# A decoder layer with a state-space scan: a new order of the work ahead of the first scan, a second chunk's front that TensorE runs four slots ahead, and gate products four scans later

## The chip, the cores and the metric

One core of one Trainium2 chip. The metric is the device time of one execution in microseconds (us), the median of several; lower is better. Engines in the profile: PE is TensorE (PEld its weight loads), DVE is VectorE, ACT is ScalarE, POOL is GpSimd, SP is SyncE, which here only issues DMAs.

## The reference, cut to what matters

The layer is a Mamba-like state-space block, a cross-attention over 1601 context rows, and a mixture of experts. The change lies in the first block alone, which computes for 2048 tokens of width 256:

```
xz = layernorm(x) @ W_in                    # 256 -> 2 x 512
x_proj, z = split(xz)
x_conv = silu(conv4(x_proj) + conv_b)       # causal, 4 taps, per channel
dt_in, B = split(x_conv @ W_x)              # 512 -> 16 + 16
dt = softplus(dt_in @ W_dt + b_dt)          # -> 512
h  = h * exp(dt * A) + dt * B * x_conv      # per token; 512 channels x 16 states
y  = h.sum(states) + x_conv * D
x  = x + (y * silu(z)) @ W_out
```

Everything is float32. The cross-attention and the experts follow, and start when this block has ended.

## The kernel before

`scan_block` cuts the 2048 tokens into four chunks of 512 (NQ). In each chunk the 512 x 16 recurrences are laid out as 64 tiles of 128 partitions x 512 tokens, so there are 256 scans in all, numbered t; one is a TENSOR_TENSOR_SCAN of VectorE (L569). Scan t needs `exp(dt*A)`, made by ScalarE into one of five PSUM banks (L466, `psA`), and the input `dt*B*x`, made by GpSimd in pairs of tiles (L298) into a ring of eight (`b_in`). Both read `rep`, in which 32 channels of dt and of u = dt*x are copied to four groups of 32 partitions by DMA: four DMAs of 128 KB for each of j = 0..3 (`spread`, L208), for every 16 scans. TensorE adds up the 16 states of a channel (`add_states`, L774, once for four scans, L771 at the first of four such groups) into the bank `psY`. After 16 scans VectorE multiplies the sum by silu(z): `gate(n)` (L526), placed after scan t with t % 16 == 2. The next group's first sum waits for the gate (`gated`), and four scans wait for the sum three groups back (`summed`), since `h` holds three groups.

The order on every engine is that of the program text; it is written by hand. Chunk q's front (normalization, transposes, the x half and the z half of W_in, convolution, x_ssm, step size, B) is cut into steps with a slot k each, and `front_time(q, k)` gives the scan t at which an engine meets the step; each engine has its own k for its part (PE_X, ACT_X, ...). Chunk 1's steps are squeezed to 3/5 slot each from t = 4 on.

Chunk 0 has no scans to hide behind and runs as a plain sequence ahead of the loop over t:

- VectorE: `moments(0)` (L497, L500), `normalize(0)` (L507), four small copies (`pick`, L534), the twelve convolution products (L540, two tiles of SBUF in, chained by a semaphore), `moments(1)`, `neg_a` (L550), then for m = 0..3 bias and -|v| (L554, L556) and, in pairs, `step_and_input` (L518, L520), which makes dt and u; then `normalize(1)`.
- ScalarE: `xnT` (L432), exp of a_log (L434), the x half's evacuations and first taps (L322, L440), silu (L444), xs (L446), exp and ln for the softplus (L450, L452), the evacuations of B (L334). The z half of chunk 0 is evacuated in the loop at t = 2, 3, 5, 6, and its silu, with two loads of activation tables, stands at t = 12 (L338).
- GpSimd: the deviation of chunk 0 (L261, L263), `conv_d` (L273), `skip_d` (L278), `pick_b` (L281), the deviation of chunk 1, and the DMAs of j = 3 of the first spread; SP issues those of j = 0, 1, 2.
- TensorE: transposes (L605), the x half of W_in (L610), x_ssm (L645), step sizes and B's products in turns through two banks (L655, L660), then the z half, then the loop.

Of the kernel before, what the change touches and what calls it, by code (L numbers as in the profile page):

```python
# [50 lines left out]
ACT_Z0, ACT_ZS0 = (2, 3, 5, 6), 12  # L51
# [64 lines left out]
def scan_block(nc, x, w, x_res, shared, following, load_next, clear_next, make_pad, ident, power, ps):  # L116
# [7 lines left out]
    with ExitStack() as ctx:  # L124
# [89 lines left out]
        def _(sp_):  # L214
            xv = x[0].rearrange("(n p) d -> p n d", p=P)
            sp_.dma_start(x_res[:, 0:CHT, :], xv[:, 0:CHT, :]).then_inc(x_in, 16)
            sp_.dma_start(w_in[:, :, 0:DI], w["W_in"][:, 0:DI].rearrange("(k p) n -> p k n", p=P)).then_inc(s_win[0], 16)
# [30 lines left out]
        def _(pool):  # L248
# [68 lines left out]
        def _(act):  # L317
# [12 lines left out]
            def evac_b(q, g):  # L330
# [159 lines left out]
        def _(dve):  # L490
            link, _n = chain(dve, dve_link, 0)

            def moments(q):
# [1339 lines left out]
```

## Time and profile before

| | us |
|---|---|
| median of 3 runs (763.28 to 764.29) | 763.36 |
| the profiled execution, whole | 771.62 |
| its span | 769.9 |
| first scan starts, from the span's start | 48.40 |
| last scan ends | 410.66 |
| VectorE busy over the span | 592.6 (77%) |
| GpSimd busy | 475.0 (62%) |
| ScalarE busy | 445.9 (58%) |
| TensorE busy | 642.0 (83%) |

The profiled execution is 8.26 us longer than the median of the runs; 1.72 us of that lie outside its span. Busy shares are means over stages with different limits, so the two stages that the change touches (up to 48.40 us, and the scans up to 410.66 us) are read by themselves. In the rows, the number in square brackets is idle time of the engine before the instruction, with what ended it.

### The profile page before, as it was taken

The numbers are of one execution on the slowest core, as the hardware profiler recorded it, in microseconds if no ns is written. First come the engines' busy times: TensorE is split into PE (matmuls) and PEld (weight loads), VectorE is DVE, ScalarE is ACT, GpSimd is POOL, SyncE is SP. The second block draws the span as 40 slices with busy tenths as digits, with TensorE's granted clock in tenths as the row PEclk, the third lists the DMA queues.
The fourth block names the chain that finished last, engine by engine and source line by source line (L and its number), as shares of the span: only waits on it lengthen the run. The fifth ranks groups of instructions, "written<-read, shape, count | busy, mean of one in ns | idle before, by whom it ended". The sixth has DMA issues, their size and how long they took to land. (4 is left out here: it accounts for less than half of the span.)

```text
span 769.9 us, 10453 instructions
## 1 busy us (share of the span) xinstructions
PE 642.0 (83%) x3130; PEld 402.0 (52%) x3130; DVE 592.6 (77%) x1040; ACT 445.9 (58%) x795; POOL 475.0 (62%) x391
## 2 busy tenths in 40 slices
PE   4589865997689964588888899999999978899991
PEld 2133212352133510044535898989998954688860
DVE  5886788889998999999887776778798876344328
ACT  2667699676987888758773445545454330344420
POOL 4169589978997999999872423333445445155650
PEclk9899995999769996588999999999999999899996
DMA  7093144315344452943323844533443132455318
GB/s 197 19 212 72 38 110 109 83 44 131 72 109 110 92 128 68 245 102 86 72 86 108 249 138 153 178 123 117 143 133 99 38 119 76 121 158 163 112 32 299
DMA packets 61604, 91.33 MB, mean 119 GB/s; under 512 B 13573, under 2 KB 46536, under 8 KB 61550
## 3 DMA queue, kind: packets, MB, share of 16 engines
q1 hardware_dynamic: 52366, 76.72, 37.8%
q0 software_dynamic: 3936, 8.72, 3.2%
q10 hardware_dynamic: 5248, 5.24, 1.9%
q8 instruction: 26, 0.43, 0.2%
q14 instruction: 28, 0.23, 0.1%
HBM read 36.54 MB, written 22.62 MB: 77 GB/s over the span
## 5 line engine op out<-in xcount | busy, mean ns | idle before, releaser
L298 POOL TENSOR_TENSOR b_in<-rep,b_rep 128x1024 f32<-128x1024 f32 x128 | 299.0, 2358 | 41.8 <-DVE h L569 34.7
L569 DVE TENSOR_TENSOR_SCAN h<-ps,hlast,b_in 128x512 f32<-128x512 f32 x256 | 306.7, 1265 | 17.2 <-ACT ps L466 10.2
L466 ACT ACTIVATE ps<-rep,neg_a 128x512 f32<-128x512 f32 x256 | 171.0, 684 | 42.5 <-DVE h L569 38.7
L774 PE MATMUL ps<-h,pick 128*32 128x512 f32 x512 | 80.8, 708 | 43.0 <-DVE h L569 42.6
L610 PE MATMUL ps<-xnT,w_in 128*128 128x512 f32 x128 | 69.3, 688 | 10.0 <-ACT xnT L352 4.1
L1081 POOL DMA_INDIRECT rows_by_token<-yt,yrow x46 | 44.7, 972 | 44.0 <-issue 26.3
L1220 DVE TENSOR_TENSOR p_lo<-ps,p_hi 128x512 fp32r<-128x512 f32 x64 | 35.2, 592 | 36.0 <-ACT p_hi L1092 34.9
L1488 PE MATMUL ps<-v_hi,p_hi 128*128 128x256 f32 x208 | 59.8, 288 | 1.2 <-DVE x_res L1343 1.2
L774 PEld LDWEIGHTS ps<-h,pick 128*32 128x32 f32 x512 | 10.7, 115 | 93.7 <-DVE h L569 83.3
L1488 PE MATMUL ps<-v_lo,p_hi 128*128 128x256 f32 x208 | 58.4, 281 | 0.0
L1488 PE MATMUL ps<-v_hi,p_lo 128*128 128x256 f32 x208 | 58.2, 280 | 0.0
L610 PEld LDWEIGHTS ps<-xnT,w_in 128*128 128x128 f32 x128 | 26.8, 220 | 52.2 <-issue 40.9
L1092 ACT ACTIVATE p_hi<-ps 128x512 fp32r<-128x512 f32 x64 | 30.0, 516 | 37.4 <-PE ps L1505 37.4
L1694 PE MATMUL ps<-w_exp,xT 128*128 x184 | 45.4, 391 | 0.0
L625 PE MATMUL ps<-xp,conv_d 128*128 128x512 f32 x96 | 43.8, 601 | 0.0
L1488 PE MATMUL ps<-c_hi,q_hi 128*128 128x512 f32 x96 | 41.0, 427 | 0.8 <-PEq L124 0.8
L1038 POOL DMA_INDIRECT rows_by_block<-xn,pos x32 | 31.9, 996 | 15.7 <-issue 10.9
L1457 DVE TENSOR_TENSOR ht<-sgt,ps 128x256 f32<-128x256 f32 x23 | 9.7, 421 | 40.5 <-ACT sgt L1185 40.5
L1062 POOL TENSOR_TENSOR attn_rstd<-attn_mv,eps 128x1 f32<-128x1 f32 x14 | 4.1, 291 | 58.3 <-DVE attn_mv L1213 58.3
L1488 PEld LDWEIGHTS ps<-v_hi,p_hi 128*128 128x128 f32 x208 | 39.1, 188 | 1.4 <-DVE x_res L1343 1.4
L1488 PEld LDWEIGHTS ps<-v_lo,p_hi 128*128 128x128 f32 x208 | 39.2, 189 | 0.0
L1488 PEld LDWEIGHTS ps<-v_hi,p_lo 128*128 128x128 f32 x208 | 39.2, 188 | 0.0
(265 smaller groups left out, 1325.8 us busy)
## 6 DMA issues: line engine op xcount, KB each, us to landing
rep<-dt_u SPq DMA_DIRECT2D x252, 128.0 KB, 2.4
mask_sb<-in_mask_BxSxS_ik_dram SPq DMA_DIRECT2D x16, 800.5 KB, 4.6
xt<-rows_by_block SPq DMA_DIRECT2D x23, 258.0 KB
rows_by_block<-pad SPq DMA_DIRECT2D x4, 1032.0 KB, 9.4
rows_by_token<-pad ACTq DMA_DIRECT2D x4, 1024.0 KB, 6.2
yb<-rows_by_token SPq DMA_DIRECT2D x4, 512.0 KB, 5.5
w_exp<-L_ffn_expert_gate_w_dram SPq DMA_DIRECT2D x15, 128.0 KB
w_exp<-n_L_ffn_expert_up_w_dram SPq DMA_DIRECT2D x15, 128.0 KB
```

The costliest lines, as they stand in the source:

```text
L298: pool.tensor_tensor(b_in[:, (t - 1) % NB:(t - 1) % NB + 2, :], u_rep[:, n % 2, j - 1:j + 1, :], b_rep[q % 2][:, g, :].unsqueeze(1).to_bro ...
L466: act.activation(psA[:, t % NDA, :], dt_rep[:, n % 2, j, :], ACT.Exp, scale=neg_a[:, k:k + 1]).then_inc(exp_ready, 1)
L569: dve.tensor_tensor_scan(h[:, QC * (s % NH) + j, :], psA[:, t % NDA, :], b_in[:, t % NB, :], hlast[:, k:k + 1], ALU.mult, ALU.add).then_in ...
L610: last = pe.matmul(psF[:, m % 2, :], w_in[:, n, part * DI + m * P:part * DI + (m + 1) * P], xnT[:, n, :], start=(n == 0), stop=(n == KE - 1))
L625: last = pe.matmul(psF[:, m % 2, :], conv_d[:, m, n, :], xp[:, m, n:n + CH], start=(n == 0), stop=(n == NTAP - 1))
L774: last = pe.matmul(psY[32 * j:32 * j + 32, :], pick[:, :], h[:, QC * (s % NH) + j, :], start=False, stop=(g == NG - 1))
L1038: pool.indirect_dma_start(xs_dram[:, :], bass.IndirectOffsetOnAxis(ap=pos[:, t, k:k + 1], axis=0), xn3[:, t, :], None, bounds_check=NTILE ...
L1081: pool.indirect_dma_start(y_dram[:, :], bass.IndirectOffsetOnAxis(ap=yrow[:, 2 * s + a:2 * s + a + 1], axis=0), yt[:, s % YT, a, :], None, ...
L1092: act.activation(p_hi[:, a:b, :], psP[g % 2][:, 0:(b - a) * P], ACT.Copy).then_inc(pthi_ready, 1)
L1220: dve.tensor_tensor(p_lo[:, a:b, :], psP[g % 2][:, 0:(b - a) * P], p_hi[:, a:b, :].bitcast(F32), ALU.subtract).then_inc(ptlo_ready, 1)
L1488: mm = pe.matmul(out, stat[a], mov[b], start=first and n == 0, stop=last and n == 2)
L1694: last = pe.matmul(psG[i % 2][:, a * 2 * FI:(a + 1) * 2 * FI], xT[:, i % 2, cols], w_all[:, ds(e, 1), wcols].rearrange("p a n -> p (a n)") ...
```

## The change

Ahead of the first scan:

- x of chunk 1 is loaded by a DMA of its own, third in SP's queue. `moments(1)`, `normalize(1)` and `neg_a` move ahead of the convolution on VectorE; GpSimd makes chunk 1's deviation ahead of `conv_d`, and waits for chunk 1's normalization before `conv_d`.
- TensorE does 36 transposes of the identity (WARM) before the first real ones.
- The z half of W_in follows the x half directly, in four banks of `psA`; its silu is taken from there by ScalarE between the silus of the convolution, so the evacuations, the silu and the two table loads of chunk 0 leave the loop.
- All four step sizes are computed in a row, into four banks. The softplus of m = 0, 1 is finished ahead of the loop; that of m = 2, 3 goes into the loop: VectorE's L554 and L556 after scans 1 and 2, ScalarE's exp and ln at t = 5 and 6, VectorE's `step_and_input` after scans 6 and 7.
- Of the first spread, SP issues two DMAs of j = 0 and those of j = 1 and 3, ScalarE two of j = 0, GpSimd those of j = 2 (after the second u). The first four inputs are made singly by GpSimd. B's four products go to four banks and are evacuated behind ScalarE's DMAs.

In the loop: chunk 1's front is placed at 7/10 slot a step from t = -4 on, and TensorE runs its steps another four slots earlier. `gate` stands after t % 16 == 6. The `after` lines of the diff use names new to it: `psV` are the four banks of the step sizes.

```diff
@@ -40,6 @@
 PE_LAST = 58
+GATE_AT = 6
...
@@ -48,7 @@
 ACT_Z, ACT_XS, ACT_BR, ACT_V, ACT_ZS = (39, 40, 42, 43), 49, (52, 53, 56, 57), (58, 60, 64, 66), 76
-ACT_Z0, ACT_ZS0 = (2, 3, 5, 6), 12
+POOL_J, PE_LEAD, WARM = 2, 4, 36
+LATE_ABS, LATE_EXP, LATE_STEP = (1, 2), (5, 6), (6, 7)
...
@@ -58,11 @@
 def front_time(q, k):
-    return 4 + k * 3 // 5 if q == 1 else TILES * (q - 1) - SHIFT + k
-def front_slots(t, first=1):
-    return [(q, k) for q in range(first, NQ + 1) for k in SLOTS if front_time(q, k) == t and (q > 1 or k >= 0)]
+    return k * 7 // 10 - 4 if q == 1 else TILES * (q - 1) - SHIFT + k
+def front_slots(t, first=1, lead=0):
+    return [(q, k) for q in range(first, NQ + 1) for k in SLOTS if front_time(q, k) == t + (lead if q == 1 else 0) and (q > 1 or k >= 0)]
...
@@ -168 @@
+        psV = [psF[:, 1, :], psF[:, 0, :], psY, psA[:, KM, :]]
...
@@ -215,6 @@
     sp_.dma_start(w_in[:, :, 0:DI], w["W_in"][:, 0:DI].rearrange("(k p) n -> p k n", p=P)).then_inc(s_win[0], 16)
+    sp_.dma_start(x_res[:, CHT:2 * CHT, :], xv[:, CHT:2 * CHT, :]).then_inc(x_next, 16)
...
@@ -227,8 @@
     sp_.dma_start(w_in[:, :, DI:], w["W_in"][:, DI:].rearrange("(k p) n -> p k n", p=P)).then_inc(s_win[1], 16)
-    sp_.dma_start(x_res[:, CHT:, :], xv[:, CHT:, :]).then_inc(x_rest, 16)
-    sp_.dma_start(w_out[:, :, :], w["W_out"].rearrange("(m p) n -> p m n", p=P)).then_inc(s_wout, 16)
+    sp_.dma_start(x_res[:, 2 * CHT:, :], xv[:, 2 * CHT:, :]).then_inc(s_rest, 16)
+    sp_.dma_start(w_out[:, :, :], w["W_out"].rearrange("(m p) n -> p m n", p=P)).then_inc(s_rest, 16)
...
@@ -238,8 @@
             sp_.wait_ge(b_ready, 16 * (n - 1))
-        for j in range(QC if n else QC - 1):
-            spread(sp_, n, j)
+        for j in range(QC):
+            if n == 0 and j == 0:
+                spread(sp_, n, j, range(0, 2))
+            elif n or j != POOL_J:
+                spread(sp_, n, j)
...
@@ -268,7 @@
     inverse_deviation(0)
-    pool.wait_ge(xn_ready, 1)
+    inverse_deviation(1)
+    pool.wait_ge(xn_ready, 2)
...
@@ -279,9 @@
     pool.tensor_copy(pick_b[:, :, :], pick[:, NS:2 * NS].unsqueeze(2).to_broadcast([P, NS, 32])).then_inc(pick_ready, 1)
-    inverse_deviation(1)
-    pool.wait_ge(u_ready, 1)
-    spread(pool, 0, QC - 1)
+    pool.wait_ge(u_ready, 2)
+    spread(pool, 0, POOL_J)
...
@@ -292,7 @@
             pool.wait_ge(rep_sem(n, j), rep_count(n, j))
-        if j % 2:
+        if t < QC:
+            pool.tensor_tensor(b_in[:, t, :], u_rep[:, 0, t, :], b_rep[0][:, 0, :], ALU.mult).then_inc(b_ready, 1)
+        elif j % 2:
...
@@ -331,7 @@
             act.wait_ge(b_ready, TILES * (q - 1))
-        act.activation(b_rep[q % 2][:, g, :], psF[:, (g + 1) % 2, :], ACT.Copy).then_inc(br_ready, 1)
+        act.activation(b_rep[q % 2][:, g, :], psF[:, (g + 1) % 2, :] if q else psA[:, g, :], ACT.Copy).then_inc(br_ready, 1)
...
@@ -439,28 @@
                        scale=conv_w[:, m, 0:1]).then_inc(tap_done, 1)
-    for m in range(KM):
+    def silu_x0(m):
         act.activation(xc[0][:, m, :], xc[0][:, m, :], ACT.Silu).then_inc(xc_ready, 1)
-    act.wait_ge(xs_ps, 1)
-    act.activation(xs[:, :], psF[:, 0, :], ACT.Copy).then_inc(xs_ready, 1)
-    act.preload_act_table_set("natural_log_exp_and_others")
-    for m in range(KM):
+    def silu_z0(m):
+        act.wait_ge(z_ps, m + 1)
+        act.activation(zs[0][:, m, :], psA[:, m, :], ACT.Silu).then_inc(z_evac, 1)
+    def log_step(m):
         act.activation(u[:, m, :], u[:, m, :], ACT.Ln, bias=1.0).then_inc(sp_ready, 1)
-        if m % 2:
-            evac_b(0, m - 1)
-            evac_b(0, m)
+    silu_x0(0)
+    silu_x0(1)
+    silu_z0(0)
+    silu_x0(2)
+    silu_z0(1)
+    silu_z0(2)
+    silu_x0(3)
+    silu_z0(3)
+    act.wait_ge(xs_ps, 1)
+    act.activation(xs[:, :], psF[:, 0, :], ACT.Copy).then_inc(xs_ready, 1)
+    act.preload_act_table_set("natural_log_exp_and_others")
+    for m in range(2):
+        log_step(m)
+    act.wait_ge(u_ready, 1)
+    spread(act, 0, 0, range(2, QC))
+    for g in range(NG):
+        evac_b(0, g)
     act.wait_ge(consts_ready, 1)
+    act.wait_ge(br_ready, NG)
             act.wait_ge(rep_sem(n, j), rep_count(n, j))
+        if t == KM:
+            act.wait_ge(v_evac, KM)
...
@@ -469,10 @@
                            h[:, QC * (e % NH):QC * (e % NH) + QC, CH - 1], ACT.Copy).then_inc(saved, 1)
-        if t in ACT_Z0:
-            evac_z(0, ACT_Z0.index(t))
-        if t == ACT_ZS0:
-            silu_z(0)
+        if t in LATE_EXP:
+            log_step(2 + LATE_EXP.index(t))
...
@@ -522,7 @@
         dve.wait_ge(summed, NG * (n + 1))
-        dve.wait_ge(zs_ready, q + 1)
+        if q:
+            dve.wait_ge(zs_ready, q)
+        else:
+            dve.wait_ge(z_evac, KM)
...
@@ -533,6 @@
     last.then_inc(pick_ready, 1)
+    moments(1)
+    normalize(1)
+    dve.wait_ge(a_exp, 1)
+    for r in range(QC):
+        rows = slice(32 * r, 32 * r + 32)
+        dst = neg_a[rows, :].rearrange("p (b g j) -> p b g j", b=KM, g=NG)
+        src = a_log[rows, :, :].rearrange("p (b j) (g n) -> p n b g j", b=KM, n=QC)[:, r]
+        last = dve.tensor_scalar(dst, src, -1.0, None, ALU.mult)
+    last.then_inc(consts_ready, 1)
...
@@ -541,23 @@
         last.then_inc(conv_done, 1)
-    moments(1)
-    dve.wait_ge(a_exp, 1)
-    for r in range(QC):
-        rows = slice(32 * r, 32 * r + 32)
-        dst = neg_a[rows, :].rearrange("p (b g j) -> p b g j", b=KM, g=NG)
-        src = a_log[rows, :, :].rearrange("p (b j) (g n) -> p n b g j", b=KM, n=QC)[:, r]
-        last = dve.tensor_scalar(dst, src, -1.0, None, ALU.mult)
-    last.then_inc(consts_ready, 1)
-    for m in range(KM):
+    def step_bias(m):
         dve.wait_ge(v_ps, m + 1)
-        dve.tensor_scalar(dt[:, m, :], psF[:, (m + 1) % 2, :], b_dt[:, m:m + 1], None, ALU.add).then_inc(v_evac, 1)
+        dve.tensor_scalar(dt[:, m, :], psV[m], b_dt[:, m:m + 1], None, ALU.add).then_inc(v_evac, 1)
         dve.scalar_tensor_tensor(u[:, m, :], dt[:, m, :], -1.0, dt[:, m, :], ALU.mult, ALU.min).then_inc(neg_abs, 1)
-        if m % 2:
-            step_and_input(m - 1)
-            step_and_input(m)
-    normalize(1)
+    step_bias(0)
+    step_bias(1)
+    step_and_input(0)
+    step_and_input(1)
...
@@ -568,7 @@
                                hlast[:, k:k + 1], ALU.mult, ALU.add).then_inc(scanned, 1)
-        if t % 16 == 2 and t > 16:
+        if t in LATE_ABS:
+            step_bias(2 + LATE_ABS.index(t))
+        if t in LATE_STEP:
+            step_and_input(2 + LATE_STEP.index(t))
+        if t % 16 == GATE_AT and t > 16:
...
@@ -652,12 @@
             pe.wait_ge(br_ready, NG * q + m + 3)
-        pe.matmul(psF[:, (m + 1) % 2, :], w_dt[:, m * P:(m + 1) * P], xs[:, :], start=True, stop=True).then_inc(v_ps, 1)
+        pe.matmul(psF[:, (m + 1) % 2, :] if q else psV[m], w_dt[:, m * P:(m + 1) * P], xs[:, :], start=True, stop=True).then_inc(v_ps, 1)
             pe.wait_ge(br_ready, NG * q + g - 1)
-        pe.matmul(psF[:, (g + 1) % 2, :], pick_b[:, QC * g:QC * g + QC, :].rearrange("p n d -> p (n d)"), xs[:, :],
+        pe.matmul(psF[:, (g + 1) % 2, :] if q else psA[:, g, :], pick_b[:, QC * g:QC * g + QC, :].rearrange("p n d -> p (n d)"), xs[:, :],
...
@@ -675,7 @@
         if k == PE_XNT:
-            pe.wait_ge(dt_ready, KM * q)
+            if q == 1:
+                pe.wait_ge(v_evac, 2)
+            else:
+                pe.wait_ge(dt_ready, KM * q)
...
@@ -776,38 @@
     pe.wait_ge(ident_ok, 2)
+    for _ in range(WARM):
+        pe.transpose(psA[:, KM, 0:P], ident[:, :], ident[:, :])
         x_part(0, m)
+    pe.wait_ge(s_win[1], 16)
+    for m in range(KM):
+        w_in_product(psA[:, m, :], m, 1).then_inc(z_ps, 1)
     small_product(0)
+    for m in range(KM):
+        step_size(0, m)
     pe.wait_ge(pick_ready, 2)
-    for m in range(KM):
-        if m == 2:
-            pe.wait_ge(br_ready, 1)
-        if m == 3:
-            pe.wait_ge(br_ready, 2)
-        step_size(0, m)
-        if m % 2:
-            pe.wait_ge(v_evac, m)
-            spread_b(0, m - 1)
-            pe.wait_ge(v_evac, m + 1)
-            spread_b(0, m)
-    pe.wait_ge(s_win[1], 16)
-    for m in range(KM):
-        if m < 2:
-            pe.wait_ge(br_ready, 4 - m)
-        else:
-            pe.wait_ge(z_evac, m - 1)
-        w_in_product(m, 1).then_inc(z_ps, 1)
+    pe.wait_ge(z_evac, KM)
+    for g in range(NG):
+        spread_b(0, g)
     pe.wait_ge(diag_ready, 2)
+    for t in range(-2 * PE_LEAD, 0):
+        for c, f in front_slots(t, 1, PE_LEAD):
+            front(c, f)
         q, k, s = t // TILES, t % TILES, t // QC
+        if t == QC:
+            pe.wait_ge(v_evac, KM)
             add_states(s - 1)
-        for c, f in front_slots(t):
+        for c, f in front_slots(t, 1, PE_LEAD):
...
```

## Rows read from the trace of the kernel before

**Rows 1.** The groups of VectorE's instructions, 48 to 400 us: count, busy, mean, idle before.
```profile
L569 DVE TENSOR_TENSOR_SCAN h<-ps,hlast,b_in 128x512 f32<-128x512 f32 x247 | 296.1, 1265 | 17.2 <-ACT ps L466 10.2 <-ACT hlast L470 3.6 <-POOL b_in L298 3.4
L526 DVE TENSOR_TENSOR zs<-ps,zs 128x512 f32<-128x512 f32 x15 | 10.1, 676 | 13.1 <-PE ps L774 13.1
```

**Rows 2.** The same view of GpSimd, 48 to 400 us.
```profile
L298 POOL TENSOR_TENSOR b_in<-rep,b_rep 128x1024 f32<-128x1024 f32 x127 | 296.6, 2358 | 41.8 <-DVE h L569 34.7 <-DMA rep<-dt_u 6.8
L314 POOL TENSOR_TENSOR dt_u<-dt_u,xc 128x512 f32<-128x512 f32 x12 | 15.2, 1267 | 4.1 <-DVE dt_u L584 4.1
```

**Rows 3.** Timeline of all engines, 0 to 62 us: start, length of the group, instruction, idle before.
```profile
4.45 1.41 DVE L497 BATCH_NORM_STATS2 stats<-x_res 128x6 f32<-128x256 f32 x4 [3.42 <-DMA x_res<-in_x_dram]
...
7.71 1.38 DVE L507 TENSOR_SCALAR xn<-x_res,mv,rstd 128x256 f32<-128x256 f32 x4 [1.45 <-POOL rstd L263]
9.01 4.99 DVE L534 COPY pick<-ident 32x32 f32<-32x32 f32 x4
9.17 3.61 POOL L273 TENSOR_TENSOR conv_d<-ident,conv_w 128x2048 f32<-128x2048 f32 x1 [1.50 <-DVE xn L507]
...
12.74 1.04 POOL L278 TENSOR_TENSOR skip_d<-ident,d_skip 128x512 f32<-128x512 f32 x1
...
14.07 0.61 POOL L281 COPY pick_b<-pick 128x512 f32<-128x512 f32 x1 [0.29 <-DVE pick L534]
...
17.72 9.04 DVE L540 SCALAR_TENSOR_TENSOR xc<-xp,conv_w,xc 128x512 f32<-128x512 f32 x12 [3.72 <-ACT xc L440]
...
27.57 1.93 PE L645 MATMUL ps<-xc,w_x 128*32 128x512 f32 x8 [6.14 <-ACT xc L444]
...
30.30 3.47 PE L655 MATMUL ps<-xs,w_dt 128*128 128x512 f32 x4 [0.80 <-ACT xs L446]
...
36.67 18.26 SPq L208 DMA_DIRECT2D rep<-dt_u  x28
...
48.40 14.21 DVE L569 TENSOR_TENSOR_SCAN h<-ps,hlast,b_in 128x512 f32<-128x512 f32 x12 [3.16 <-POOL b_in L298]
```

**Rows 4.** TensorE in one stretch: stretch and length, busy, granted clock, DMA share, GB/s.
```profile
27.00:28.00 1.00, 0.43 (x4) 0.50 0.00 0
```

**Rows 5.** From issue to landing: the spreads (36 to 62 us), then W_in's two halves.
```profile
DMA to landing us min/median/max: 2.4/3.6/5.4
...
DMA to landing us min/median/max: 4.8/4.9/5.0
```

**Rows 6.** VectorE's waits, 48 to 98 us, last row 98 to 130: total, times, longest.
```profile
DVE h L569 <- ACT ps L466: 4.9, 3, 3.7
DVE h L569 <- ACT hlast L470: 3.6, 1, 3.6
...
DVE zs L526 <- PE ps L774: 1.9, 1, 1.9
...
DVE dt_u L584 <- ACT dt_u L385: 4.9, 3, 2.5
```

**Rows 7.** Timeline, 60 to 98 us: tables and silu on ScalarE, TensorE's x_ssm product.
```profile
62.13 1.28 ACT L338 ACT_TABLE_LOAD   x1
...
96.77 1.04 PE L645 MATMUL ps<-xc,w_x 128*32 128x512 f32 x8
```

**Rows 8.** Timeline behind the scans: a GpSimd instruction beside and without VectorE's L1315.
```profile
424.74 2.33 DVE L1315 TENSOR_TENSOR v_lo<-v_all,v_hi 128x1024 fp32r<-128x1024 f32 x2
...
424.90 1.08 POOL L1062 TENSOR_TENSOR attn_rstd<-attn_mv,eps 128x1 f32<-128x1 f32 x1 [4.86 <-DVE attn_mv L1213]
...
462.54 0.19 POOL L1062 TENSOR_TENSOR attn_rstd<-attn_mv,eps 128x1 f32<-128x1 f32 x1 [4.18 <-DVE attn_mv L1213]
```

**Rows 9.** Timeline around three gates, VectorE and TensorE, from 145 to 362 us.
```profile
156.22 0.69 DVE L526 TENSOR_TENSOR zs<-ps,zs 128x512 f32<-128x512 f32 x1 [4.81 <-PE ps L774]
...
183.58 1.06 PE L774 MATMUL ps<-h,pick 128*32 128x512 f32 x8 [1.68 <-DVE h L569]
...
351.40 1.91 PE L771 MATMUL ps<-xc,skip_d 128*128 128x512 f32 x2
```

More of the change, by code:

```diff
@@ L169, in scan_block @@
         psA = ps[:, 3 * BANK:8 * BANK].rearrange("p (s n) -> p s n", s=NDA)
+        psV = [psF[:, 1, :], psF[:, 0, :], psY, psA[:, KM, :]]
         psL = [psF[:, 0, 0:DM], psF[:, 1, 0:DM]] + [psA[:, t % NDA, 0:DM] for t in (TILES * NQ - 5, TILES * NQ - 4)]
-        x_in, x_rest, s_win, s_small, s_zero, s_alog = sem("x_in"), sem("x_rest"), [sem("w_x_in"), sem("w_z_in")], sem("small_in"), sem("zeroed"), sem("alog_in")
+        x_in, x_next, s_win, s_small, s_zero, s_alog = sem("x_in"), sem("x_next"), [sem("w_x_in"), sem("w_z_in")], sem("small_in"), sem("zeroed"), sem("alog_in")
         pick_ready, diag_ready = sem("pick_ready"), sem("diag_ready")
-        s_conv, s_wout = sem("conv_in"), sem("w_out_in")
+        s_conv, s_rest = sem("conv_in"), sem("rest_in")
         ident_ok = sem("ident_ok")
@@ L200, in rep_sem, with spread @@
         def rep_sem(n, j):
-            return rep_pool if n == 0 and j == QC - 1 else rep_in[n % 2][j]
+            return rep_pool if n == 0 and j == POOL_J else rep_in[n % 2][j]
         def rep_count(n, j):
-            return (n // 2 + (0 if j == QC - 1 and n % 2 == 0 and n else 1)) * QC * 16
-        def spread(eng, n, j):
-            for r in range(QC):
+            return (n // 2 + (0 if j == POOL_J and n % 2 == 0 and n else 1)) * QC * 16
+        def spread(eng, n, j, rows=range(QC)):
+            for r in rows:
                 eng.dma_start(rep[32 * r:32 * r + 32, n % 2, j, :, :],
@@ L493, in moments @@
             def moments(q):
-                dve.wait_ge(x_in if q == 0 else x_rest, 16)
+                dve.wait_ge(*((x_in, 16), (x_next, 16), (s_rest, 32))[min(q, 2)])
                 dve.wait_ge(xn_ready, q)
@@ L543, in _ @@
                 last.then_inc(conv_done, 1)
-            moments(1)
-            dve.wait_ge(a_exp, 1)
-            for r in range(QC):
-                rows = slice(32 * r, 32 * r + 32)
-                dst = neg_a[rows, :].rearrange("p (b g j) -> p b g j", b=KM, g=NG)
-                src = a_log[rows, :, :].rearrange("p (b j) (g n) -> p n b g j", b=KM, n=QC)[:, r]
-                last = dve.tensor_scalar(dst, src, -1.0, None, ALU.mult)
-            last.then_inc(consts_ready, 1)
-            for m in range(KM):
+            def step_bias(m):
                 dve.wait_ge(v_ps, m + 1)
-                dve.tensor_scalar(dt[:, m, :], psF[:, (m + 1) % 2, :], b_dt[:, m:m + 1], None, ALU.add).then_inc(v_evac, 1)
+                dve.tensor_scalar(dt[:, m, :], psV[m], b_dt[:, m:m + 1], None, ALU.add).then_inc(v_evac, 1)
                 dve.wait_ge(v_evac, m + 1)
                 dve.scalar_tensor_tensor(u[:, m, :], dt[:, m, :], -1.0, dt[:, m, :], ALU.mult, ALU.min).then_inc(neg_abs, 1)
-                if m % 2:
-                    step_and_input(m - 1)
-                    step_and_input(m)
-            normalize(1)
+            step_bias(0)
+            step_bias(1)
+            step_and_input(0)
+            step_and_input(1)
             for t in range(TILES * NQ):
@@ L606, in normal, with w_in_product @@
                 last.then_inc(xnT_ps, 1)
-            def w_in_product(m, part):
+            def w_in_product(out, m, part):
                 for n in range(KE):
-                    last = pe.matmul(psF[:, m % 2, :], w_in[:, n, part * DI + m * P:part * DI + (m + 1) * P], xnT[:, n, :],
+                    last = pe.matmul(out, w_in[:, n, part * DI + m * P:part * DI + (m + 1) * P], xnT[:, n, :],
                                      start=(n == 0), stop=(n == KE - 1))
@@ L619, in x_part @@
                     pe.wait_ge(x_evac, m - 1)
-                w_in_product(m, 0).then_inc(x_ps, 1)
+                w_in_product(psF[:, m % 2, :], m, 0).then_inc(x_ps, 1)
             def convolve(q, m):
@@ L629, in project @@
                 pe.wait_ge(gated, KM * (q + 1))
-                pe.wait_ge(s_wout, 16)
+                pe.wait_ge(s_rest, 32)
                 for m in range(KM):
@@ L694, in front @@
                         pe.wait_ge(c_evac, 3 + m)
-                    w_in_product(m, 1).then_inc(z_ps, 1)
+                    w_in_product(psF[:, m % 2, :], m, 1).then_inc(z_ps, 1)
                 if k == PE_XS:
```

1 line of the change is left out of this document (removed).

## The prediction, written before the result was known

> **What bounds the kernel now.** The page's busy shares name no one engine, so the reader goes to the two stages that the change touches. The timeline of the first 62 us is a chain of single engines: normalization, convolution on VectorE from 17.72 to 26.76, x_ssm on TensorE at 27.57, step sizes at 30.30, then SP's first spread DMA at 36.67, where the first u is ready (36.64), and the first scan at 48.40, 11.76 us behind that u [rows 3]. From there to 410.66 us the groups by engine show VectorE at 296 us of scans and GpSimd at 297 us of inputs in 352 us [rows 1, 2]. GpSimd's idle time is 34.7 us of waiting for scans, so VectorE sets the pace; its spacing is 14.21/12 = 1.18 us a scan [rows 3]. What it loses is idle time: 13.1 us before gates, for TensorE's sums, 13.8 us for ScalarE before scans [rows 1]. The waits by stretch put 10.4 us of the loss between scans 8 and 24 (4.9 + 3.6 + 1.9) and 4.9 us, before the step sizes of chunk 1, between scans 37 and 42 [rows 6]. All else behind the scans shifts with them.
>
> **The sum** is made against the profiled execution, 771.62 us; the median is 8.26 lower.
>
> **1. Up to the first u: +0.9 us (0 to +1.8 as forecast, -3.9 if nothing collides).** VectorE's order becomes: copies, moments and normalization of chunk 1, neg_a, convolution. x of chunk 1 is issued third; W_in's half, issued just ahead of it, takes at most 5.0 us to land [rows 5], so it is there at about 8 us, ahead of its use. Moments start at about 9.6 us, and from moments to the normalization's start it takes 7.71 - 4.45 = 3.26 us, the normalization 1.38 [rows 3]: done at 14.2. neg_a (0.9 us, an estimate from the kernel's page of groups) ends at 15.1. Were the first taps ready then (TensorE is kept busy ahead by 36 transposes, and the x half's first product took twice the time of the later ones), the twelve convolution products, 9.04 us [rows 3], would end at 24.2 instead of 26.76.
>
> But conv_d now starts only when chunk 1 is normalized, at 14.3, and so runs to 17.9, with skip_d (1.04) and pick_b (0.61) behind it, beside the convolution; before they were over at 14.7, ahead of it [rows 3]. Does VectorE run beside GpSimd? A copy of 32x32 elements beside conv_d did not: four of them took 4.99 us while conv_d and skip_d ran [rows 3]. And GpSimd's L1062, 0.19 us alone, took 1.08 us when VectorE had a product of two SBUF tiles under way [rows 8]. The convolution's products read two SBUF tiles each. No row shows such a product waiting for GpSimd, so the bounds are no wait (end at 24.2) and a wait for all three instructions (17.9 + 1.65 + 9.04 = 28.6). I take the second, being nearest to both rows: +1.8 us.
>
> The Trainium skill (SBUF — State Buffer, "Who interferes with whom") says that a VectorE instruction with two SBUF inputs contends with a GpSimd instruction that reads SBUF, and that whichever came first holds the port for its whole length. By that rule the end is 28.6; without it 24.2. The rows agree with it from GpSimd's side.
>
> Behind the convolution, ScalarE's silu order puts chunk 0's z between, which is ready by then and costs nothing: the silu that x_ssm waits for comes when the last convolution block does. TensorE now has the z products to fill the wait; its x_ssm products ran at 0.5 granted clock (the 1.2 GHz level) after 6.14 us idle [rows 3, 4] and took 1.93 us, against 1.04 us later [rows 7]; the first step size took 1.73 (two of L655) where half would do. If the clock stays up, that is -0.9 - 0.9 = -1.8; TensorE is idle about 4 us instead of 6, so I take half: -0.9. Sum +0.9: the first u at 37.5.
>
> **2. From the first u to scan 8: +9.2 us (+2.6 to +10).** The first scan comes sooner. Before, scan 0 stood at u + 11.76. Now four DMAs of j = 0 go out on two queues at once, the first landing 2.4 us after its issue, four at about 4.6 (the fastest and the median of the spreads [rows 5] leave 3.6 to 5.4); one single input is 1.27 (as L314 [rows 2]): scan 0 at u + 6.0, a gain of 5.8. It is given back at once: all 16 DMAs still need until about u + 11, since they are as many bytes, so scans 1 to 3 wait for landings, two bias steps (2 x 1.4) fill the gaps, and scan 4 stands at u + 16.4, where it was before (u + 16.5). Then two step_and_input calls, 2.8 us, lie in the path after scans 6 and 7: scan 8 at u + 23.9 against u + 21.3. That is the lower end, +2.6. Each call has two products of two SBUF tiles with a semaphore between, GpSimd is in its pairs of 2.36 us, back to back, and up to eight inputs ahead; if each of the four lets one pair pass, or nearly (one finds GpSimd waiting), plus 0.7 for the bias step of m = 3, it is 2.36 x 2.5 + 0.7 = 6.6 more: u + 30.5. I take that, by the same reading as in step 1. Behind these waits: ScalarE and TensorE are ahead of VectorE there and gain room.
>
> **3. Scans 8 to 24: -10.4 us (-6.8 to -10.4).** The table load at 62.13 [rows 7] opens the z half's silu, 4.5 us with two loads, in the loop; it goes, and with it the 4.9 us of waits for ps. The gate that waited 1.9 us for TensorE stands four scans (4.7 us) later. The 3.6 us before scan 24 came when ScalarE, late for want of TensorE's convolution, did its own silu; TensorE is four slots ahead now. If only ScalarE's work counts, these 3.6 stay.
>
> **4. Scans 24 to 64: -1.6 us (0 to -3).** 7/10 slot a step gives ScalarE's step sizes 6 scans where they had 5: of 4.9 us of waits about 3.3 remain.
>
> **5. The gates from scan 64 on: -3.2 us (+6.1 to -11.2).** 13.1 - 1.9 = 11.2 us of gate waits lie there, 4.81 of them at one [rows 1, 9]. The gate four scans later covers each, but TensorE is busy without a break from 134 to 182 us, and ends with only 1.68 us to wait for VectorE [rows 9]: what the gate gains is lost before the residuals that need the same TensorE. So 1.7 us there, 0.4 in the next chunk, 1.1 at the last two gates.
>
> Sum: 0.9 + 9.2 - 10.4 - 1.6 - 3.2 = -5.1 us; 771.6 - 5.1 = 766.5 for a profiled execution, 758.3 for the median. I say 758.0.
>
> **The rivals.**
>
> A, nothing collides: VectorE's two-tile products run beside GpSimd. For it: no row shows them waiting. Against: rows 8, seen from the other side. Steps 1 and 2 are then -3.9 (2.6 us earlier convolution and 1.3 of clock, TensorE having no gap) and +2.6: 763.4 - 3.9 + 2.6 - 10.4 - 1.6 - 3.2 = 746.9. Chance 0.15.
>
> B, the later gate holds TensorE, which decides where TensorE and not VectorE sets the pace. Its sum of the next group waits for the gate; before, TensorE came to that point at 351.40, 2.3 us after the gate [rows 9]; four scans later the gate ends at 354.5, so TensorE loses 3.1 us there, and by the same reckoning 1.7 at scan 86 and 1.3 at scan 118. If these 6.1 us pass to the end in place of step 5's gain, the sum is 763.4 - 1.9 + 6.1 = 767.6, slower than before. For it: TensorE is the late one at five gates. Against: behind 351.40 TensorE waits for ScalarE anyway. Chance 0.13.
>
> C, chunk 1's front is bound by ScalarE, whatever slots it gets: step 3 gives 6.8 and step 4 nothing. 763.4 + 0.9 + 9.2 - 6.8 - 3.2 = 763.5. For it: ScalarE has 0.69 us of exp a scan and some 31 us of front in 64 scans, nearly VectorE's time. Against: silu and z of chunk 0, 6.8 us, leave it. Chance 0.13.
>
> The forecast has 0.59, with its own range 751 to 763. A difference below 0.2% (1.5 us) can't be told from none. Faster: 0.15 of A, 0.55 of the forecast, 0.05 of the others, 0.75; same: 0.10, most of it C; slower 0.15, B and what of the forecast meets with C. The range, 747 to 765, leaves out half of A and most of B.
>
> **What would show it.** In the new trace: conv_d at 14 us and the convolution's first product not before 17.9, its last at about 28.5 (A: first at 15, last at 24); x_ssm's eight products in about 1.0 us if the clock held; first scan at 43.5, with gaps before scans 1 to 3; the products of L518's step after scans 6 and 7 with 1 to 2.4 us of waiting each (A: none), scan 8 at about 68; no table load between 40 and 75 us and no gate that waits over 1 us; new waits of the residuals behind scans 73 and 137; TensorE idle before the first sum after each gate, 3 us or more. The first scan later than 48, or TensorE still late at the end of the block, would make the prediction wrong.

## The result and the profile after

The changed kernel takes **776.95 us** (median of 4 runs, 775.45 to 778.79), the kernel before 763.83 beside it: ratio **1.0146**, 95% interval [1.0123, 1.0169]. The two medians lie 13.1 us apart, the ratio is worth 11.2 us: slower, where 5 us less was forecast. The profiled execution is 778.79 us long, its span 777.1.

The first scans of successive groups, from timelines of VectorE, show where the time went (us; the last column is the change of the stretch):

| scan | before | after | stretch | change | forecast |
|---|---|---|---|---|---|
| 0 | 48.40 | 44.80 | | | |
| 8 | 57.83 | 70.04 | start to 8 | +12.2 | +10.1 |
| 24 | 88.19 | 89.83 | 8 to 24 | -10.6 | -10.4 |
| 64 | 147.43 | 146.94 | 24 to 64 | -2.1 | -1.6 |
| end of 255 | 410.66 | 421.11 | 64 to end | **+10.9** | **-3.2** |

The stretch behind the last scan is 359.2 us in the profile before and 355.9 after. Its code is unchanged, and it differs between the profiles of this case (352.9 to 362.5 us), so positions of scans are compared below where a few us matter, and medians for verdicts.

**From scan 64 on.** VectorE's waits from 147 us to the last scan: total, times, longest.

```profile
DVE x_res L542 <- PE ps L670: 11.4, 6, 2.8
DVE h L603 <- ACT ps L496: 8.9, 9, 1.7
DVE dt_u L622 <- ACT dt_u L394: 6.4, 4, 3.2
```

The same view of the kernel before, 147 to 411 us:

```profile
DVE zs L526 <- PE ps L774: 11.2, 4, 4.8
DVE h L569 <- ACT ps L466: 4.3, 6, 1.7
DVE dt_u L584 <- ACT dt_u L385: 2.0, 3, 1.2
```

The gate waits of [rows 1] are gone. In their place stand the residuals (11.4 us), and VectorE's waits for ScalarE are 9 us larger: 27.4 us of waiting in all instead of 17.5. TensorE's own waits over the same stretch (150 to 421 us) name what made the projections and step sizes late:

```profile
PE ps L812 <- DVE zs L557: 36.9, 9, 6.9
PE ps L815 <- DVE h L603: 20.6, 10, 4.8
```

Before it was 5.3 us in 4 waits (the line below, of that kernel's TensorE, 147 to 411 us). TensorE starts a group's sum with two skip_d products (L812) into the one bank that the gate reads. They wait for the gate, and TensorE runs in order.

```profile
PE ps L771 <- DVE zs L526: 5.3, 4, 2.2
```

One such chain, in timelines of TensorE, ScalarE and VectorE of the changed kernel, 290 to 304 us (start, length of the group, instruction, idle before):

```profile
293.35 2.08 PE L812 MATMUL ps<-xc,skip_d 128*128 128x512 f32 x2 [5.78 <-DVE zs L557]
...
297.22 2.07 PE L693 MATMUL ps<-xs,w_dt 128*128 128x512 f32 x2
...
300.33 1.12 PE L693 MATMUL ps<-xs,w_dt 128*128 128x512 f32 x2
```
```profile
299.33 0.69 ACT L389 ACTIVATE dt_u<-ps,b_dt 128x512 f32<-128x512 f32 x1 [3.39 <-PE ps L693]
...
301.15 0.63 ACT L394 ACTIVATE dt_u<-dt_u 128x512 f32<-128x512 f32 x1
```
```profile
292.63 0.67 DVE L557 TENSOR_TENSOR zs<-ps,zs 128x512 f32<-128x512 f32 x1
...
301.81 0.69 DVE L622 TENSOR_TENSOR dt_u<-ps,dt_u 128x512 f32<-128x512 f32 x1 [3.20 <-ACT dt_u L394]
```

The step-size product needed nothing from the gate, but stood behind the sum that did. In the kernel before the same sum, L771, had waited 0.49 us, with the gate at 285.46:

```profile
286.18 1.12 PE L771 MATMUL ps<-xc,skip_d 128*128 128x512 f32 x2 [0.49 <-DVE zs L526]
...
295.13 2.08 PE L655 MATMUL ps<-xs,w_dt 128*128 128x512 f32 x2
```

Is TensorE's clock a second loss? Behind the 5.78 us of idle time the two L693 products took 2.07 us at a granted clock of 0.50 (the 1.2 GHz level, 293 to 299 us), the next two of the same shape 1.12 at 1.00 (300 to 304 us). But the kernel before pays this too: its granted clock is 0.50 from 293 to 333 us, and two such products (L655, above) take 2.08. From scan 64 on its mean is 0.85 (150 to 411 us), that of the changed kernel 0.87 (150 to 421 us). So the lower clock is no part of what the change adds there.

**The front.** VectorE, 14 to 50 us:

```profile
14.15 5.40 DVE L574 TENSOR_SCALAR neg_a<-a_log 32x64 f32<-32x64 f32 x4
19.58 9.04 DVE L580 SCALAR_TENSOR_TENSOR xc<-xp,conv_w,xc 128x512 f32<-128x512 f32 x12
...
37.63 0.69 DVE L548 TENSOR_TENSOR dt_u<-dt_u,xc 128x512 f32<-128x512 f32 x1
...
44.80 1.28 DVE L603 TENSOR_TENSOR_SCAN h<-ps,hlast,b_in 128x512 f32<-128x512 f32 x1 [5.03 <-POOL b_in L303]
49.71 1.28 DVE L603 TENSOR_TENSOR_SCAN h<-ps,hlast,b_in 128x512 f32<-128x512 f32 x1 [3.63 <-ACT ps L496]
```

GpSimd in the same stretch, then TensorE's x_ssm products:

```profile
14.31 3.61 POOL L281 TENSOR_TENSOR conv_d<-ident,conv_w 128x2048 f32<-128x2048 f32 x1 [1.50 <-DVE xn L535]
17.88 1.04 POOL L286 TENSOR_TENSOR skip_d<-ident,d_skip 128x512 f32<-128x512 f32 x1
18.87 0.61 POOL L289 COPY pick_b<-pick 128x512 f32<-128x512 f32 x1
```
```profile
29.43 1.57 PE L683 MATMUL ps<-xc,w_x 128*32 128x512 f32 x8 [4.16 <-ACT xc L454]
```

VectorE around the late calls, 60 to 71 us, where GpSimd is in its pairs:

```profile
60.07 2.75 DVE L546 SCALAR_TENSOR_TENSOR dt_u<-dt_u 128x512 f32<-128x512 f32 x1
62.85 2.73 DVE L548 TENSOR_TENSOR dt_u<-dt_u,xc 128x512 f32<-128x512 f32 x1
...
66.70 0.66 DVE L546 SCALAR_TENSOR_TENSOR dt_u<-dt_u 128x512 f32<-128x512 f32 x1
67.39 2.73 DVE L548 TENSOR_TENSOR dt_u<-dt_u,xc 128x512 f32<-128x512 f32 x1
70.04 2.45 DVE L603 TENSOR_TENSOR_SCAN h<-ps,hlast,b_in 128x512 f32<-128x512 f32 x2
```
```profile
57.60 7.43 POOL L307 TENSOR_TENSOR b_in<-rep,b_rep 128x1024 f32<-128x1024 f32 x3
66.92 2.65 POOL L307 TENSOR_TENSOR b_in<-rep,b_rep 128x1024 f32<-128x1024 f32 x1 [1.89 <-DVE h L603]
```

The lost time shows as length, not as idle time: three of the four products last 2.7 us instead of 0.69, so a view of waits alone would miss 6.1 us. Each long product began while a pair of GpSimd's was under way and ends 0.55 us behind it (65.58 and 70.12 behind pairs that end at 65.03 and 69.57). The short one began at 66.70, with GpSimd idle until 66.92.

### The profile page after: what moved, and what is told of

Same layout as the page of the kernel before. It is cut to its first block and busy times, and to the rows that moved or that the text cites. A ratio compares the mean times of both kernels' runs of the same rounds, so it can differ in the third digit from the quotient of the medians.

```text
span 777.1 us, 10520 instructions
## 1 busy us (share of the span) xinstructions
PE 639.0 (82%) x3166; PEld 404.5 (52%) x3166; DVE 600.0 (77%) x1040; ACT 439.9 (57%) x792; POOL 478.2 (62%) x393
## 5 line engine op out<-in xcount | busy, mean ns | idle before, releaser
L815 PE MATMUL ps<-h,pick 128*32 128x512 f32 x512 | 78.1, 692 | 25.5 <-DVE h L603 25.2
L648 PE MATMUL ps<-xnT,w_in 128*128 128x512 f32 x128 | 65.7, 660 | 14.2 <-ACT zs L337 6.0
L812 PE MATMUL ps<-xc,skip_d 128*128 128x512 f32 x32 | 23.1, 811 | 37.7 <-DVE zs L557 37.7
L815 PEld LDWEIGHTS ps<-h,pick 128*32 128x32 f32 x512 | 11.4, 116 | 75.2 <-DVE h L603 57.3
L1076 POOL DMA_INDIRECT rows_by_block<-xn,pos x32 | 32.4, 1012 | 11.1 <-issue 10.5
```

Source lines behind the costliest of these rows:

```text
L648: last = pe.matmul(out, w_in[:, n, part * DI + m * P:part * DI + (m + 1) * P], xnT[:, n, :], start=(n == 0), stop=(n == KE - 1))
L815: last = pe.matmul(psY[32 * j:32 * j + 32, :], pick[:, :], h[:, QC * (s % NH) + j, :], start=False, stop=(g == NG - 1))
L1076: pool.indirect_dma_start(xs_dram[:, :], bass.IndirectOffsetOnAxis(ap=pos[:, t, k:k + 1], axis=0), xn3[:, t, :], None, bounds_check=NTILE ...
```

## The experiments

Theory G: the gate's place alone makes the change slow, by holding TensorE's next sum. Its rival: the front does it, through later chunks that start from another state. Theory L: the late calls of the front lose to GpSimd's pairs. Ratios are against the kernel before, timed on the same chip. Its median beside them was 765.6 us for the first four runs below and 768.3 to 768.6 for the others, so ratios and positions are compared, not times.

### The kernel before once more, and the gate alone

> The kernel before, unchanged, for a second profile of it, since the first one's execution lay 8 us above its median. If the part behind the scans varies between executions, the last scan ends at 410 to 411 us again and only the stretch behind it is shorter, by about 8 us. If the scans themselves varied, the last scan ends near 403.

764.53 us, span 762.8, last scan done at 408.72 with 354.07 behind it. The first profile had 410.66 and 359.23: of the 7.1 us between the two spans 5.2 lie behind the scans and 1.9 ahead of their end. The stretch from scan 24 to 64 alone took 57.1 us, 59.2 in the first profile: by this second profile the changed kernel's 57.1 is no gain. What causes either difference stays open.

```
-                if t % 16 == 2 and t > 16:
+                if t % 16 == 6 and t > 16:        (in the kernel before, nothing else)
```

> The kernel before with its gate products after t % 16 == 6 instead of 2, nothing else. Theory G (the later gate holds TensorE's next sum, and what stands behind it in its order, about three scans longer): all of the loss behind scan 64 comes back, scan 64 to the last one takes 10 to 11 us more than before, the residuals behind scans 73, 137 and 201 wait 2 to 3 us, the time is about 773 to 775. Rival F (the loss is chunk 1's new placement or the new order ahead of the scans, and the gate is neutral or gains as forecast): 760 to 764.

780.04 us, ratio 1.0191 [1.0164, 1.0218]. VectorE's and TensorE's waits, 147 to 422 us:

```profile
DVE x_res L514 <- PE ps L632: 11.4, 6, 2.8
DVE h L569 <- ACT ps L466: 8.8, 9, 1.6
DVE dt_u L584 <- ACT dt_u L385: 6.3, 4, 3.2
```
```profile
PE ps L771 <- DVE zs L526: 37.0, 9, 6.9
```

These are the changed kernel's four rows, to 0.1 us, with the old front. From scan 64 to the last it takes 273.9 us, the kernel before 263.2, the changed one 274.2. Theory G holds, its rival falls. The time was forecast 5 us too low (773 to 775): the kernel before was 2.2 us longer beside this run than the forecast took it, 1.6 us more stand ahead of scan 64 (149.05 against 147.43), the rest is not placed. The mean granted clock from scan 64 on is 0.86, that of the kernel before 0.85.

### The new front with the old gate, and one scan later

```
-GATE_AT = 6
+GATE_AT = 2        (and 3 in the second)
```

> The changed kernel with the gate put back to t % 16 == 2. Theory G: scans 64 to the last as before, no waits of the residuals, waits at the gates again; with scan 64 about where it was, about 763 (761 to 765). Rival F: 775 to 778, as the changed kernel.

766.26 us, ratio 1.0009 [0.9994, 1.0024]: with the gate where it was, the front is worth nothing that can be measured. (761 to 765 had been forecast.) From scan 64 to the last it takes 263.5 us again.

> The changed kernel with the gate after t % 16 == 3. TensorE's next sum needs scan 3 in any case, so theory G prices this hold at the gate's own 0.6 us a gate, some of it hidden, against one scan (1.2 us) of cover for each of the five gates that waited 1.8 to 4.8 us: 1 us either side of the kernel with the gate after 2. If the gate's place costs in proportion to its distance from 2 (a quarter of 11 us), it is 2 to 3 us slower than that one.

764.78 us, ratio 0.9988 [0.9975, 1.0001]. Waits of VectorE, 145 to 406 us:

```profile
DVE zs L557 <- PE ps L815: 5.9, 4, 3.6
DVE h L603 <- ACT ps L496: 3.6, 5, 1.5
DVE x_res L542 <- PE ps L670: 2.5, 3, 1.0
DVE dt_u L622 <- ACT dt_u L394: 2.0, 3, 1.2
```

The sum is 14.0 us. With the gate at 2 the gates had waited 12.4; of the 6.5 that go, 2.5 come back at the residuals. The median is 1.5 us below that of the gate at 2, where 1 us either way was forecast.

> The kernel before with its gate after t % 16 == 3, nothing else: what one scan of cover is worth by itself. By the kernel with the new order, where it took 1.5 us off, 763.5 to 765 against some 765.5.

768.12 us, ratio 0.9993 [0.9971, 1.0014], last scan at 407.98. The gate at 3 gains nothing measurable with the old front, where up to 2 us had been forecast: 2 us fewer waits (15.6 against 17.5) are below what the timing can tell.

### The late calls moved out of the scans

From here on the gate stands at 3 where nothing else is said. The remaining bias steps go right behind step_and_input(1), ScalarE's log_step(2), (3) behind B's evacuations, and step_and_input(2), (3) behind scan 0, where GpSimd waits for landings.

```
             step_and_input(1)
+            step_bias(2)
+            step_bias(3)
...
-                if t in LATE_STEP:
-                    step_and_input(2 + LATE_STEP.index(t))
+                if t == 0:
+                    step_and_input(2)
+                    step_and_input(3)
```

> The kernel with the new order and the gate after 3, but the step sizes of m = 2, 3 not late: VectorE's bias steps directly behind the second u, ScalarE's exp and ln behind B's evacuations, both step_and_input calls behind scan 0, while GpSimd waits for the DMAs. Theory L (a VectorE product of two SBUF tiles waits for the GpSimd instruction that has begun, 2 to 2.6 us each): scan 0 at 44.5 and scan 1 at 49 as before, no product above 0.8 us, scan 8 at 59 instead of 69.3. Rival O (only the late products' own 0.7 us each are on the path): scan 8 at 66. At the end 759 to 762 by theory L, for part of the 10 us is taken back by waits for chunk 1's front up to scan 64.

764.7 us, ratio 0.9954 [0.9935, 0.9973]. VectorE, 45 to 60 us:

```profile
46.70 0.66 DVE L546 SCALAR_TENSOR_TENSOR dt_u<-dt_u 128x512 f32<-128x512 f32 x1
47.40 0.69 DVE L548 TENSOR_TENSOR dt_u<-dt_u,xc 128x512 f32<-128x512 f32 x1
48.01 0.68 DVE L546 SCALAR_TENSOR_TENSOR dt_u<-dt_u 128x512 f32<-128x512 f32 x1
48.73 1.64 DVE L548 TENSOR_TENSOR dt_u<-dt_u,xc 128x512 f32<-128x512 f32 x1
```

The four products take 3.7 us instead of 8.9, scan 8 stands at 59.80 instead of 69.31 (59 against 66 were the forecasts): L holds. One product took 1.64 us where none above 0.8 was forecast: GpSimd had begun a single input at 48.37, and the product ends 0.55 us behind it. Of the 9.5 us only 3.1 are left at scan 64 (142.57 against 145.65) and 1.4 at the last scan. Scans 8 to 24 take 25.8 us instead of 19.4, with 5.8 us of waits for ScalarE and TensorE: these had gained room behind the long products, and are the late ones again.

### conv_d ahead of chunk 1's deviation, neg_a and pick behind the convolution

```
-            inverse_deviation(1)
-            pool.wait_ge(xn_ready, 2)
+            pool.wait_ge(xn_ready, 1)
             ... conv_d ...
+            inverse_deviation(1)
...                    (on VectorE, neg_a and the four copies move behind the twelve products)
```

> The kernel with the new order and the gate after 3, but with conv_d back ahead of chunk 1's deviation on GpSimd (at about 9 us), neg_a and the pick copies behind the convolution on VectorE, skip_d and pick_b after them. Theory L: chunk 1's normalization ends at 15.3 instead of 14.2, the convolution starts there instead of 19.6 and ends at 24.4 instead of 28.6, TensorE has no gap ahead of x_ssm; first u at 33 to 34 instead of 38, everything up to scan 64 some 4 us earlier: 760 to 762. Rival S (what stands ahead of the first scan is given back by scan 64, since chunk 1's front needs its time anyway): scan 64 moves by under 1.5 us, 763 to 765.

763.43 us, ratio 0.9921 [0.989, 0.9952]. VectorE, 15 to 26 us:

```profile
15.22 9.03 DVE L569 SCALAR_TENSOR_TENSOR xc<-xp,conv_w,xc 128x512 f32<-128x512 f32 x12
24.16 0.86 DVE L578 TENSOR_SCALAR neg_a<-a_log 32x64 f32<-32x64 f32 x4
25.06 0.73 DVE L582 COPY pick<-ident 32x32 f32<-32x32 f32 x4
```

With GpSimd silent, neg_a takes 0.86 us instead of 5.40, the four copies 0.73 instead of 4.99 [rows 3], and x_ssm's products 1.07. The first scan comes 5.6 us sooner than with the gate at 3 alone, scan 64 5.8: what is gained ahead of the first scan is kept, and rival S (under 1.5 us at scan 64) falls.

> The kernel with the gate at 3, and neg_a alone moved on VectorE from ahead of chunk 0's convolution to behind it; GpSimd still has conv_d, skip_d and pick_b from 14.3 to about 19.5 us. In the changed kernel neg_a's four instructions held VectorE for 5.4 us (14.15 to 19.55). Theory S, the port: it is GpSimd's block that holds whatever VectorE has next, so the convolution's first product begins no earlier than 17.9, its last ends at 28 to 28.6 as before the edit, neg_a (0.9 us) comes behind it, and the time is that of the gate at 3 (764.8) within 1.5 us. Theory N: neg_a with its strided source is the one kind that waits, and products of two SBUF tiles run beside GpSimd: convolution from 14.2 to about 23.5, first scan at 39.5 to 40.5, median 760 to 761.

This one is that kernel with GpSimd's block in place and neg_a alone behind the convolution: 767.52 us, ratio 0.9988 [0.9965, 1.0011]. The convolution's twelve products: min, median, max.

```profile
L573 DVE SCALAR_TENSOR_TENSOR xc<-xp,conv_w,xc x12: 737/752/3624, 14.8 to 26.8; 128x512 f32<-128x512 f32 x12
```

The first product lasts 3.62 us: it began at 14.79, with conv_d under way until 17.87. The second and third take 1.41 and 0.98, beside skip_d and pick_b, which get longer too (1.49 for 1.04, 1.07 for 0.61); the other nine run at their 0.75. The last product ends at 27.6, not at the forecast 28 or more. So theory S is right in kind: VectorE's two-tile product waits out the GpSimd instruction that began first, and then the two take turns. Theory N's 23.5 is excluded. The ratio is that of the gate at 3 alone, 0.9988.

### Both, and what the other parts are worth

> Both edits, the late steps early and conv_d early, with the gate after 3. If they add up, 755 to 758; if chunk 1's front on ScalarE and TensorE bounds scans 16 to 64, the second edit brings its 4 us (a shift of everything) and the first little more: 758 to 760.

756.94 us, ratio **0.985** [0.9824, 0.9876], the lowest median of all: scan 0 at 39.37, scan 8 at 53.67, scan 64 at 135.88, the last done at 395.87. The two edits do more than add up: at the last scan they bring 1.4 and 5.9 us alone, 9.8 together.

The next three each change one constant (or one placement) of it:

```
-GATE_AT = 3
+GATE_AT = 4
```

> The kernel with both orders mended (756.9) and the gate at 4 in place of 3. Theory G: TensorE's next sum waits for psY until the gate is done, and residuals, step sizes and projections queue behind it; with the gate at 3 some gates wait themselves (up to 3.6 us) and residual waits are 1.04, 1.04 and 0.42; at 6 the loss was 11 to 14 us over three chunks. At 4 the gate stands 1.2 us later than at 3, the gates wait less and the residuals more, both about 1 us a chunk: median within 2.5 us of 756.9 on the slow side, 757 to 759.5. Rival: the loss is a threshold between 3 and 6 where another operation (the residual at scans 73 and 137) changes place, and all 11 us come already at 4: 766 or more.

757.96 us, ratio 0.9861 [0.9842, 0.988], last scan done at 395.78. 757 to 759.5 had been forecast, and there is no threshold between 3 and 4; their intervals overlap, so 3 and 4 are not told apart. VectorE's waits, 135 to 396 us, and TensorE's for the gate:

```profile
DVE x_res L542 <- PE ps L671: 4.7, 5, 1.3
DVE zs L557 <- PE ps L816: 3.7, 3, 1.9
DVE h L605 <- ACT ps L498: 3.2, 5, 1.4
DVE dt_u L623 <- ACT dt_u L394: 2.1, 3, 1.3
```
```profile
PE ps L813 <- DVE zs L557: 18.8, 8, 4.5
```

| gate at | TensorE waits for gates | the longest | gates wait | residuals wait | VectorE's waits in all |
|---|---|---|---|---|---|
| 2 (before) | 5.3 | 2.2 | 11.2 | 0 | 17.5 |
| 3 | 10.6 | 3.3 | 5.9 | 2.5 | 14.0 |
| 4 | 18.8 | 4.5 | 3.7 | 4.7 | 14.2 |
| 6 | 36.9 | 6.9 | 0 | 11.4 | 27.4 |

All from scan 64 to the last, in us. The first row has the old front; with the new one and the gate at 2 the figures are 5.2, 2.2, 12.4, 0 and 17.9. The longest hold grows by 1.2 us, one scan's time, for each scan that the gate is moved.

```
-POOL_J, PE_LEAD, WARM = 2, 4, 36
+POOL_J, PE_LEAD, WARM = 2, 4, 0
```

> The kernel with both orders mended (756.9 measured) and none of the 36 warm-up transposes ahead of the first normalization's. If the granted clock at x_ssm comes from how busy TensorE was since 2.4 us, the first x half products run at the 1.2 GHz level and the convolution may start up to 1 us later; later stages keep their clock since z fills the wait. I expect the first scan 0.5 to 1.5 us later and a median of 757 to 758.5. Rival: the x half is not on the path (moments and normalization of chunk 1 stand between on VectorE until 14.2) and nothing changes, 756.9.

760.4 us, ratio 0.99 [0.9861, 0.9939]. TensorE's first work, with and without the warm-up:

```profile
9.11 1.09 PE L644 MATMUL ps<-ident,xn 128*128 128x128 f32 x8 [0.18 <-DVE xn L535]
11.40 10.97 PE L649 MATMUL ps<-xnT,w_in 128*128 128x512 f32 x25 [1.21 <-ACT xnT L441]
```
```profile
9.04 1.94 PE L644 MATMUL ps<-ident,xn 128*128 128x128 f32 x8 [9.04 <-DVE xn L535]
12.18 10.34 PE L649 MATMUL ps<-xnT,w_in 128*128 128x512 f32 x19 [1.21 <-ACT xnT L441]
```

The transposes take 1.94 us instead of 1.09, and the x half's first four products 3.75 us, where nine took 4.10; the convolution starts at 17.51 instead of 15.33, the first scan is 2.7 us later, and 2.1 us are left at the last scan. I had expected 0.5 to 1.5 us. The positions show it; the four times (757.85 to 763.48) scatter, and the interval overlaps that of the kernel with the warm-up. That the slower products ran at a lower clock is inferred from their lengths: the granted clock that the profile gives for 8 to 20 us is 1.00 in both.

```
-    return k * 7 // 10 - 4 if q == 1 else ...
+    return 4 + k * 3 // 5 if q == 1 else ...        (and PE_LEAD = 0)
```

> The kernel with both orders mended (756.9) and chunk 1's front placed as in the kernel before (slot 4 + 3k/5, TensorE no slots ahead). The prediction put 3.3 to 3.6 us of its steps 3 and 4 down to the new placement (waits of the scans before 24 and at 37 to 42); the rest of step 3 (6.8) to z's silu leaving the loop. If that holds, scan 64 stands 3 to 6.5 us later than 135.88 and the median is 760 to 763. Rival: with z out of the loop ScalarE has room wherever the front stands, scan 64 within 1 us, median 757 to 758.

766.4 us, ratio 0.9957 [0.9939, 0.9975]; scan 64 6.8 us later, all of it between scans 8 and 24 (31.8 us instead of 25.0), the last scan 8.3. One wait of 3.97 us before scan 24 comes back:

```profile
85.35 3.63 DVE L605 TENSOR_TENSOR_SCAN h<-ps,hlast,b_in 128x512 f32<-128x512 f32 x3 [3.97 <-ACT hlast L502]
```

It is the 3.6 us wait of [rows 6], with z's silu out of the loop already. So the placement of chunk 1's front, TensorE's lead included, is a gain of its own in this kernel, larger than the 3 to 6.5 us that I gave it, and rival C's assumption (it is ScalarE's load, whatever the slots) fails.

## Why the prediction was wrong

- **Step 1, up to the first u: nearly right in size, partly wrong in its place.** +0.9 forecast, +1.7 measured (38.3). The convolution ended at 28.6 as forecast, by luck: what waited for GpSimd was neg_a, costed at 0.9 and 5.40 long, though [rows 3] had four small copies held in the same way; the products ran undisturbed behind it. Nor is "a wait for all three instructions" what products alone do: with neg_a away the block cost them 3.8 us (12.80 from first to last against 9.04). x_ssm's products took 1.57 us, between the two prices.
- **Step 2, first u to scan 8: right in kind, 1.3 us too small.** u + 30.5 forecast, u + 31.7 measured, a change of +10.5 where +9.2 was forecast and +10 was the bound; the first scan at u + 6.5. Three of four products waited, and scan 4 stood at u + 18.2, not 16.4. The trace has 2.73 us beside GpSimd's pairs, 0.69 without, and moving them gave 9.5 us back at scan 8. Rival A is excluded. This agrees with the rule that the prediction took from the Trainium skill (SBUF — State Buffer, "Who interferes with whom").
- **Step 3, scans 8 to 24: the number is right (-10.6 for -10.4), in part by luck.** With the late calls moved away the same stretch takes 25.8 us, 4.6 less than before: some 6 of the 10.6 us are there because ScalarE and TensorE caught up while VectorE sat in step 2's long products. Nor does its split hold (6.8 us for z's silu, 3.6 for the slots): with z's silu gone and the old slots, the stretch had 11.5 us of waits, the kernel before 10.4, and the new slots were worth 6.8 us.
- **Step 4, scans 24 to 64: not shown.** -2.1 for -1.6, but two profiles of the kernel before differ by 2.2 us in this very stretch (59.2 and 57.1; 57.1 after), and the old slots cost 0.1 us there.
- **Step 5 failed**, and with it the sign: -3.2 forecast, +10.9 measured. Its sentence "the gate four scans later covers each" is true, no gate waits. "What the gate gains is lost before the residuals" held for chunk 1's gates: 4.8 us of gate wait became 4.1 us there. What the step left out is that the gate also releases TensorE's next sum. I had this as rival B with 6.1 us, but took it only at three gates and against it the sentence that "TensorE waits for ScalarE anyway". The trace shows nine holds, 36.9 us; and ScalarE waited for TensorE at the place in question (3.39 us before L389): the dependence ran in a circle, gate, sum, step-size product, step size, scan. At 0.13, rival B was the right mechanism at about half its price: with +10.9 in place of its 6.1, and the measured -0.5 in place of -1.9, its sum is 763.4 - 0.5 + 10.9 = 773.8 instead of 767.6. The 3.2 us from there to the median are no larger than what executions of one kernel differ by ahead of scan 64 (1.7 us) and behind the scans (5.2 us).
- **The sign of it could be read before.** The view of TensorE's waits of the kernel before, from scan 64 on, lists 5.3 us in four waits for the gate, 2.2 the longest, with the gate at 2. A hold that is there already gets further delay in full: the longest went 2.2, 3.3, 4.5, 6.9 us with the gate at 2, 3, 4, 6, a scan's 1.18 us for each scan. And new holds come: four, five, eight, nine.

## What to carry to other kernels

A wait that is taken from one engine by a later consumer is paid by whoever needs the buffer that the consumer frees: before moving a consumer, list the producer's waits for it, and everything queued behind that producer in its in-order engine. If both directions wait already (here 11.2 and 5.3 us), a move has little to give: one scan later was worth 0.2% with the new front and nothing measurable with the old, four scans cost 1.4 to 1.9%. A second bank might serve both directions; it was not tried. Sums of steps hide that time lost in one is caught up in the next: 9.5 us at scan 8 were 1.4 us at the last scan. And look for lost time in the lengths of instructions as well as in the idle time between them.

## What the runs showed of the hardware

- Small VectorE instructions wait for GpSimd as large ones do. neg_a (32x64 elements, strided source) took 5.40 us in four beside conv_d, 0.86 with GpSimd silent; the 32x32 copies 4.99 and 0.73. Neither has two tensors of SBUF as inputs. One by one neg_a's four took 0.20 us (begun at 14.15, ahead of conv_d's 14.31), then 3.63, 0.98 and 0.55: the last three each wait out one instruction of GpSimd's (3.61, 1.04 and 0.61 us). The Trainium skill (SBUF — State Buffer, "Who interferes with whom") names copy and tensor_scalar among the operations that can take the port pair shared with GpSimd; the prediction used only its sentence on two inputs, and costed neg_a at its undisturbed 0.9 us. By that other sentence of the Trainium skill neg_a is held wherever GpSimd has the pair first: the trace agrees (the four end at 19.55, pick_b at 19.48).
- Behind 5.78 us of idle time TensorE's granted clock stood at 0.50 (the 1.2 GHz level): two products took 2.07 us, the next two, at 1.00, 1.12. A slow product behind a wait is no sign of what a change costs, though: the kernel before had 40 us at 0.50 in the same place, and a mean of 0.85 from scan 64 on, against 0.87.
- Executions of one kernel differ in the stretch behind the scans by up to several us: 359.2 and 354.1 us in two profiles of the kernel before. No experiment was made on it.
